# Three of four state blocks leave VectorE: scaled by ScalarE, added by accumulating transfers that GpSimd issues

## The reference

```
h_s[d, t] = exp(delta[d, t] * A[d, s]) * h_s[d, t-1] + delta[d, t] * u[d, t] * B[t, s]
y[t, d]   = sum over s of C[t, s] * h_s[d, t]  +  u[t, d] * D[d]
```

## Time and profile before

| | us |
|---|---|
| median of 3 runs | 3368.53 (3368.17 to 3368.85) |
| the profiled execution, its own time | 3364.8 |
| its span, first to last instruction | 3362.8 |
| of this, `layers` | about 2785 |
| a turn in the middle (one batch) | about 162.6 |
| GpSimd busy over the span | 2592.0 (77%) |
| VectorE busy over the span | 2546.5 (76%) |
| ScalarE busy over the span | 2064.1 (61%) |

### The profile page before, as it was taken

One profiled execution on the slowest core, in us unless ns is written; L12 is line 12 of the kernel. 1 busy time (PEld: TensorE's weight loads), 2 busy tenths in 40 slices (PEclk: granted clock), 3 DMA queues, 4 the chain that ended last, 5 costly groups with the idle time before them and its releaser, 6 DMA issues. The chain is left out here.

```text
span 3362.8 us, 46770 instructions
## 1 busy us (share of the span) xinstructions
PE 2834.9 (84%) x12696; PEld 1870.1 (56%) x12697; DVE 2546.5 (76%) x4108; ACT 2064.1 (61%) x3786; POOL 2592.0 (77%) x2474
## 2 busy tenths in 40 slices
PE   3686979797979797888888888888887779999998
PEld 2444555555555555555555555565545447777776
DVE  3498989899989989898999898989897842222222
ACT  3576677676767676766767676767665514444443
POOL 1399898989889898989898989898999913444444
PEclk7897989898989898989999999999998889999999
DMA  2001111111111111111110101010112313333333
GB/s 75 23 32 32 36 44 36 43 39 39 39 39 41 38 39 40 46 33 46 34 51 26 51 29 51 29 48 31 43 36 82 101 56 58 63 63 63 62 62 52
DMA packets 113898, 155.37 MB, mean 46 GB/s; under 512 B 15472, under 2 KB 73264, under 8 KB 113712
## 3 DMA queue, kind: packets, MB, share of 16 engines
q1 hardware_dynamic: 77344, 109.32, 10.4%
q0 software_dynamic: 25728, 34.75, 6.4%
q10 hardware_dynamic: 10640, 9.09, 0.8%
HBM read 107.36 MB, written 45.76 MB: 46 GB/s over the span
## 5 line engine op out<-in xcount | busy, mean ns | idle before, releaser
L872 POOL TENSOR_TENSOR dbu<-du,bbc 128x512 f32<-128x512 f32 x1024 | 1294.2, 1279 | 74.5 <-DVE h L1440 67.8
L1440 DVE TENSOR_TENSOR_SCAN h<-bank,dbu 128x512 f32<-128x512 f32 x1024 | 1227.3, 1212 | 158.7 <-ACT bank L1082 101.9
L1082 ACT ACTIVATE bank<-region,amat 128x512 f32<-128x512 f32 x1024 | 703.6, 691 | 313.3 <-DVE h L1440 299.0
L665 PE MATMUL bank<-ident,h 128*128 128x128 f32 x4096 | 624.9, 289 | 259.5 <-DVE acc L1430 231.4
L665 PEld LDWEIGHTS bank<-ident,h 128*128 128x128 f32 x4096 | 495.6, 148 | 544.3 <-DVE acc L1430 224.7
L858 POOL TENSOR_TENSOR acc<-acc,hTc 128x512 f32<-128x512 f32 x480 | 609.6, 1271 | 103.7 <-ACT hTc L1066 102.1
L1607 POOL DMA_INDIRECT out<-ye,ids x136 | 213.3, 1569 | 347.1 <-DMA out<-ye,ids 311.3
L1066 ACT ACTIVATE hTc<-bank,cT 128x512 f32<-128x512 f32 x480 | 327.3, 682 | 236.6 <-PE bank L665 236.5
L1430 DVE SCALAR_TENSOR_TENSOR acc<-bank,cT,acc 128x512 f32<-128x512 f32 x544 | 395.0, 730 | 38.9 <-PE bank L665 33.4
L619 PE MATMUL bank<-x4T,w_su 128*128 128x512 f32 (+1 forms) x768 | 389.2, 610 | 10.7 <-DVE score L1305 10.7
L1643 DVE SCALAR_TENSOR_TENSOR gg<-gt,bank 128x352 f32<-128x352 f32 x136 | 70.7, 520 | 382.2 <-ACT gt L1577 382.2
(11 more groups left out here) (204 smaller groups left out, 4361.1 us busy)
## 6 DMA issues: line engine op xcount, KB each, us to landing
bbc<-b_scratch SPq DMA_DIRECT2D x256, 256.0 KB, 3.1
xe<-slots_in SPq DMA_DIRECT2D x136, 129.0 KB
region<-in_x SPq DMA_DIRECT2D x16, 512.0 KB, 3.8
out<-x ACTq DMA_DIRECT2D x16, 512.0 KB, 3.1
region<-in_e_gu SPq DMA_DIRECT2D x8, 704.0 KB, 5.4
out<-ye,ids POOLq DMA_INDIRECT x136
slots_in<-dbu SPq DMA_DIRECT2D x16, 129.0 KB, 3.2
slots_in<-x,pos POOLq DMA_INDIRECT x128
```

What stands on the lines that cost most here:

```text
L665: last = tr(scan[f"hT{s}.{t}"][:, m * P:(m + 1) * P], h[:, s % 2, m, t * P:(t + 1) * P], ident[:, :])
L872: g.tensor_tensor(dbu[:, n % 4, :], du[:, m, :], bbc[:, (b * NS + s) % NROW, :], ALU.mult).then_inc(S("dbu_ready"), 1)
L1082: f(db(n)[:, :], delta[:, 1 - par, m, :], ACT.Exp, scale=amat[:, m, s:s + 1]).then_inc(S("da_ready"), 1)
L1440: v.tensor_tensor_scan(h[:, s % 2, m, :], db(n)[:, :], dbu[:, n % 4, :], 0.0, ALU.mult, ALU.add)\
```

## The change

`POOLED` now holds t = 1, 2 and 3 of the first 15 states: 45 blocks a batch in place of 30. VectorE keeps 19: t = 0 of each state and the whole last state. What GpSimd does for a pooled block is no longer an addition but the issue of a DMA that reads `hTc` and adds it to `acc[:, t, :]` in SBUF. Its completion is counted by a semaphore for each of the two `hTc` buffers, and all that waited for the addition on GpSimd (ScalarE's refill of the buffer, the next addition to the same block, TensorE's transposes of `acc`) now waits for the landing.

```
-POOLED = [(s, t) for s, t in ADDS if t % 2 == 1 and s < NS - 1]
+POOLED = [(s, t) for s, t in ADDS if t > 0 and s < NS - 1]

+        acc_added = [sem(f"acc_added{k}") for k in range(2)]
+        PER_BUFFER = [(len(POOLED) + 1 - k) // 2 for k in range(2)]
+
+        def added(eng, b, k):
+            count = b * PER_BUFFER[k % 2] + k // 2 + 1
+            eng.wait_ge(acc_added[k % 2], 16 * count)

 acc_before:
             elif (s - 1, t) in POOLED:
-                done(eng, "acc_added", b, POOLED.index((s - 1, t)))
+                added(eng, b, POOLED.index((s - 1, t)))

 TensorE, ahead of the transposes of acc:
-                        done(pe, "acc_added", b)
+                        for k in range(2):
+                            pe.wait_ge(acc_added[k], 16 * (b + 1) * PER_BUFFER[k])

 GpSimd, add_scaled:
                     acc_before(pool, b, s, t)
-                    g.tensor_tensor(acc[:, t, :], acc[:, t, :], hTc[:, k % 2, :], ALU.add).then_inc(S("acc_added"), 1)
+                    g.dma_start(acc[:, t, :], hTc[:, k % 2, :], accum_op=ALU.add).then_inc(acc_added[k % 2], 16)

 ScalarE, scale_state:
-                    before(act, "acc_added", b, k - 1)
+                    if b + k // 2:
+                        act.wait_ge(acc_added[k % 2], 16 * (b * PER_BUFFER[k % 2] + k // 2))
                     f(hTc[:, k % 2, :], scan[f"hT{s}.{t}"][:, :], ACT.Copy, scale=cT[:, par, t, s:s + 1]).then_inc(S("scaled"), 1)
```

More of the change, by code:

```diff
@@ L272, in layers @@
                    b_stored=1, cT_ready=1, da_ready=UNITS, dbu_ready=UNITS,
-                   scan_done=UNITS, acc_init=TT, acc_ready=len(KEPT), scaled=len(POOLED), acc_added=len(POOLED), y3_ready=MC,
+                   scan_done=UNITS, acc_init=TT, acc_ready=len(KEPT), scaled=len(POOLED),  y3_ready=MC,
                    x3_ready=2, x4_ready=1, x4T_ready=DC, lexp_ready=1, sg1_ready=1, sg_ready=1, tag_ready=1, pos_ready=1, tok_set=1, weight_set=1,
```

## The result

The changed kernel takes 3608.37 us (median of four runs, 3607.37 to 3609.51) against 3368.69 us before: 1.0712 times as long, 95% interval 1.0696 to 1.0727, or 240 us slower. The forecast was 3578 us. The profiled execution has a span of 3605.9 us, 243.1 us more than before.

The account below looks back on a forecast made before the run. GpSimd and VectorE, nearly full, took turns at binding; after the change GpSimd alone: 114.0 + 45 x 1.27 = 171.2 us, plus 3.9 of waits, 175.1 a middle turn. Together +209 us gave 3578 us, range 3270 to 3900 (likeliest case 3390 to 3745).

Parts of the forecast that it names:

- signs of being right: In the profile: issues 1.27 us start to start, middle turns 175 us, GpSimd's waits below 5 us, long VectorE `dbu` waits.
- rival 3: The two `hTc` buffers bind: 135 us a turn at a 4.8 us landing, binding from 6.6 us; chance 0.08.
- 114.0 us of other work: GpSimd's occupied time a turn without its 30 additions: 150.9 - 36.9 us.
- X: GpSimd's time for issuing one transfer, 45 a turn: taken as 1.27 us, between 0.32 and 1.87.
- no change at X = 0.98: The issue price on GpSimd at which the kernel's time would stay the same: 0.98 us.
- The waits kept: GpSimd alone binds, so a third of its 11.7 us of waits a middle turn stays: 3.9 us.
- The wait at t = 3: ScalarE waits for the landing of t = 1: hidden; without cover about 1 us a state, 15 a turn.
- lead of four steps: GpSimd may be four steps ahead of VectorE's scan; five steps, 13 us, cover a loop of 7.4 us.
- The last turn: Turn 15, where some 2.9 us of GpSimd's idle time are waits: +18.3 us.
- the end of each batch: VectorE's last blocks wait for two landings, some 6 us later: taken as hidden, otherwise 96 us at most.
- Rival 1: GpSimd's issue is cheap and VectorE binds: at 0.6 us an issue, 160 us faster, 3208 us; chance 0.26.
- the first reading: In middle turns GpSimd (150.9 us) and VectorE (152.3 us) take turns at binding; relieving one helps as far as the other allows.

Follow-up runs that it names:

- add45: The kernel before with 45 pooled blocks in place of 30, still added by GpSimd's own additions: 3550.49 us.
- noring45: The changed kernel with transfers reading a constant tile instead of `hTc`, so ScalarE waits for no landing: 3492.26 us.
- token45: The kernel before with 45 pooled blocks, GpSimd adding only 4 of 512 columns of each: 3372.54 us.
- token30: The kernel before with its own 30 pooled blocks, GpSimd adding only 4 of 512 columns: 3336.43 us.
- lag6 runs: token45, dma30 and the changed kernel with three `hTc` buffers, each with scaling and adding one step later: 3530.31, 3842.31 and 3651.21 us.
- dma30: The changed kernel with the 30 pooled blocks of before, still added by transfers: 3412.14 us.

## Why the prediction came out right, and where it didn't

The verdict, slower, and the time (3578 for 3608) are right. The way there is right in its frame and wrong in its two largest terms, which cancel. That the time came out so near is luck. Of its own signs of being right, the issue of 1.27 us, the waits of GpSimd below 5 us and the long waits of VectorE for `dbu` failed, and what it listed as the sign of rival 3, ScalarE waiting for landings while GpSimd idles, appeared.

**The frame.** The ledger "114.0 us of other work and X an issue" held: add45 gives 168.8 us against the 169.4 that it forecasts, and after, three buffers and thirty blocks give X = 0.95, 0.94 and 0.94. Middle turns came to 175.5 us, forecast 175.1.

**The size of X.** It was taken as 1.27 us from the plain indirect transfer and is 0.95. The row that it was taken from has an index list and no second source; why the direct form is cheaper was not tried. On 45 issues this is 14.4 us a turn too much. That is the first term mis-sized. The expected sign of no change at X = 0.98 was wrong too: at 0.95 the sum would have said 22 us faster. (By the prediction's own 72 us for each 0.1 us of X, its figure for X = 1.0 is 3384 us, not 3388.)

**The waits kept.** "GpSimd alone binds, so most of its waits go" failed: 18.7 us a turn are left, not 3.9, 14.8 us too little. Where they come from, noring45 tells: without any wait of ScalarE for landings GpSimd still waits 14.0 us. So some 5 of the 14.8 us belong to the landings and some 10 have another cause. It may be the floor that token45 shows at 164.5 us a turn: at 156 to 157 us of its own work GpSimd stands below it, and at 168.8 us (add45) its waits do fall to 4.8. No run tests that link by itself. The two errors cancel to 0.4 us. A reader of the sum alone would have called it confirmed; only the list of waits tells otherwise.

**The wait at t = 3.** The prediction named the place, ScalarE waiting for the landing of t = 1 with exp and the scan behind it, priced it at 15 us a turn without its cover, and took it as hidden by GpSimd's lead of four steps. ScalarE waited 17.1 us a turn for landings. What this cost the turn is less: 5.0 us, the difference to noring45 (175.5 and 170.5). The landing was even better than forecast, 3.5 us for 4.3 to 4.8, and the DMA share 0.51 for 0.57. What failed is the lead. GpSimd issues its transfers between its `dbu` in a fixed order. At its step n it issues the transfer of block n-7, which ScalarE scales at ScalarE's step n-2, so it can be at most two steps ahead of ScalarE, whatever its lead on the scan might be. The trace shows it waiting there:

```profile
1057.81 0.87 POOL L865 DMA_DIRECT2D acc<-hTc  x1 [1.10 <-ACT hTc L1074]
1058.41 1.57 POOL L879 TENSOR_TENSOR dbu<-du,bbc 128x512 f32<-128x512 f32 x1
...
1061.51 0.88 POOL L865 DMA_DIRECT2D acc<-hTc  x1 [1.53 <-ACT hTc L1074]
```

An engine that waits for ScalarE between its own steps can't run away from it. The loop is closed: GpSimd waits for the scaling, the scaling for the landing of an earlier issue, which GpSimd gave when it had got its scaling. Rival 3 was this loop, priced for a turn that it fills (135 us at L = 4.8) and so dismissed as long as that is below 175. It never filled the turn, but it cost 116 us all the same, as three buffers and noring45 show. By the first `du` of each batch in the two profiled executions, some 65 of about 120 us lie in the thirteen middle turns, 12 in turn 0, 6 in turn 14 and 38 in the last.

**The last turn** was forecast at +18.3 us and is +47.7, which is 29 of the 30 us by which the forecast fell short. In noring45 it is about 148 us and not 185. Here weights of the experts share the DMA engines, and landings reach 9.6 us; in all turns before the longest is 5.3. The prediction looked at the end of each batch for its hidden cost, 96 us at most, and not at this neighbour. At the end of a batch little was lost: VectorE waited for landings 21.2 us in thirteen turns.

```profile
DVE acc L1438 <- DMA acc<-hTc: 21.2, 14, 2.4
```

**The other engines.** "VectorE busy 137 us with long waits for `dbu`" is half wrong: it is busy 141.0 us a turn and waits for exp on ScalarE. Turns 0 and 14 came to +12.4 and +13.0 for +15.5 and +14.6. The expert stage is unchanged, as said.

**Rival 1** was given 0.26 for a cheap issue and a gain of 160 us. token45 shows that it could not have come: with an addition of 0.2 us the kernel stands at 3372.54. The step that fails there is the first reading, that two nearly full engines take turns at binding and relief of both is paid out. Relief of both (token45), at the price of 15 more scalings on ScalarE, pays nothing; relief of GpSimd alone (token30) pays 33 us of 514. VectorE relieved without more work for ScalarE wasn't tried.

**Where the 240 us are**, from one kernel to the next: 45 blocks instead of 30, with the adding for nothing, +4 (3372.5); issues of 0.94 us in place of it, +120 (3492.3, noring45); waiting for landings with two buffers, +116 (3608.4). The second figure holds more than GpSimd's own time: it includes whatever the transfers do to the other engines, on which see below, and the granted clock, which is 0.94 over token45's turns and 0.91 over noring45's. What the clock is worth here wasn't tried apart.

**Open.** What sets the floor of 161 to 164 us a turn isn't settled. The lag6 runs point to the two PSUM banks together with the fixed order of the steps, but that isn't shown: the kernel's eight banks are all in use, and another sharing of them wasn't tried, nor were four `hTc` buffers.

## What to carry to other kernels

When an operation is replaced by a transfer, count two prices: the time the issuing engine is held (here 0.95 us in place of 1.23), and the time until the landing for which the source buffer is held (3.5 us in place of 1.27), and add a buffer before anything else. An engine can't cover a wait by its lead if its own order makes it wait each step for the engine that it is to cover. Before costing a relief, make the relieved operation nearly free and time that: here one such run (token45) would have shown that there was nothing to win.

## What the runs showed of the hardware

A direct accumulating transfer of 128 rows of 2 KB from SBUF to SBUF holds GpSimd 0.95 us by the sum of a turn (0.92 by the ends of the transfers), a plain one 0.63. Half the rows take 0.03 us off the recorded issue. The prediction weighed the Trainium skill, page "DMA: Bandwidth & Descriptors", section "Anatomy of one DMA", which calls descriptor generation small and variable; the trace doesn't show that part alone, but GpSimd is held for more than half a microsecond in either form.

A small VectorE operation with both inputs in SBUF, once a turn, got many times longer in the changed kernel. Before:

```profile
L1345 DVE TENSOR_TENSOR ohb<-ohb,slot x16: 216/298/557, 388.9 to 2737.6; 128x64 f32<-128x64 f32 x16
```

and after:

```profile
L1353 DVE TENSOR_TENSOR ohb<-ohb,slot x16: 215/1868/1952, 407.6 to 2980.7; 128x64 f32<-128x64 f32 x16
```

With thirty blocks its median is 2.49 us, with three buffers 2.70, with plain copies 0.88, with the token addition 0.22. But it doesn't take a transfer to make it long. In add45, where GpSimd adds by itself, the times scatter and the longest is longer than any of these:

```profile
L1345 DVE TENSOR_TENSOR ohb<-ohb,slot x16: 213/393/6519, 403.0 to 2923.1; 128x64 f32<-128x64 f32 x16
```

All sixteen take 41.5 us together in add45, 28.0 in the changed kernel and 4.9 before. The Trainium skill, page "SBUF — State Buffer", section "Who interferes with whom", has a VectorE instruction with two inputs in SBUF contend with a GpSimd instruction that reads SBUF. The trace agrees in kind, with add45 more than with the transfers; that the port is the cause wasn't tested by itself. The sixteen cost at most some 37 us in a kernel. In dma30 they take 36.3 us, 31 more than before, which may be part of the 43 us that it lost.
